# Macaron stack on one core: norms by log and exp inside the tick, rows turned one tick later, and a distance setup that overlaps its stacking

## The reference, cut to what matters

```python
Q = (x @ W_k.T).reshape(B, S, H, dk).transpose(0, 2, 1, 3)
squared_dist = sq_norm - 2.0 * dot + sq_norm.transpose(0, 1, 3, 2)
attn = softmax(-squared_dist * inv_sqrt_dk)
...
# one local layer, 8 heads of 64, windows of 64 that look one window back
q, k, v = split(shift_token(x) @ wqkv)
q = l2norm(q) * qs                  # l2norm: t / max(|t|, 1e-12)
k = l2norm(k) * ksc
q, k = rotary_xpos(q, k)            # rotation by position, with a growth
x = x + local_attention(q, k, v) @ wo
h = layernorm(shift_token(x)) * lg + lb
a, g = split(h @ w1 + b1)
x = x + (a * gelu(g)) @ w2 + b2
```

## Time and profile before

| | us |
|---|---|
| median of 3 runs | 3577.19 (3571.36 to 3577.69) |
| the profiled execution: its time | 3580.72 |
| its span in the trace | 3578.6 |
| TensorE, matmuls, busy | 3183.2 (89%) |
| VectorE, busy | 1976.4 (55%) |
| ScalarE, busy | 2167.5 (61%) |
| GpSimd, busy | 1737.4 (49%) |
| mean granted TensorE clock | 0.959 of full |

### The profile page before, as it was taken

How to read it: one execution, slowest core, us unless ns; L and a number is a source line. 1 busy time by engine, 2 the same in 40 slices (tenths; PEclk the granted TensorE clock), 3 DMA queues, 4 the chain that set the end, 5 groups by cost and what they waited for, 6 DMA issues and landing times. The chain is left out here.

```text
span 3578.6 us, 73165 instructions
## 1 busy us (share of the span) xinstructions
PE 3183.2 (89%) x26564; PEld 1951.8 (55%) x26564; DVE 1976.4 (55%) x4014; ACT 2167.5 (61%) x3580; POOL 1737.4 (49%) x1412
## 2 busy tenths in 40 slices
PE   6499999868999999749999999999998599999995
PEld 5222222435666666526666666666665366666663
DVE  4200000337777777545556555656565577777773
ACT  2399999526666666535555555555554366666663
POOL 1100000039889988523333333333332698998882
PEclk9699999979999999979999999999999799999998
DMA  1122222021111111100000000000000211111111
GB/s 33 20 36 39 36 38 38 7 74 34 35 36 38 37 36 34 25 10 9 7 6 9 6 9 6 9 6 9 6 6 4 86 37 35 37 37 37 35 33 36
DMA packets 124405, 95.70 MB, mean 27 GB/s; under 512 B 80448, under 2 KB 100544, under 8 KB 123968
## 3 DMA queue, kind: packets, MB, share of 16 engines
q1 hardware_dynamic: 122784, 89.41, 11.4%
q10 hardware_dynamic: 1440, 3.80, 0.3%
HBM read 22.90 MB, written 2.10 MB: 7 GB/s over the span
## 5 line engine op out<-in xcount | busy, mean ns | idle before, releaser
L1761 POOL TENSOR_SCALAR e<-e,inv 128x768 f32<-128x768 f32 (+7 forms) x512 | 375.3, 746 | 761.8 <-DVE inv L1653 761.8
L1724 ACT ACTIVATE e<-e,nmax 128x768 f32<-128x768 f32 (+7 forms) x512 | 395.4, 772 | 429.5 <-DVE e L1648 426.2
L1648 DVE TENSOR_SCALAR_CACHE_REDUCE e<-slot 128x768 f32<-128x768 f32 (+7 forms) x512 | 376.2, 754 | 243.8 <-PE slot L1537 243.8
L530 ACT ACTIVATE e<-slot 128x1024 f32<-128x1024 f32 x512 | 472.9, 1091 | 43.8 <-PE slot L466 43.8
L896 POOL TENSOR_TENSOR inv_norm<-floored,minus_half 128x16 f32<-128x16 f32 x128 | 374.1, 2922 | 10.7
L1641 DVE COPY eT<-slot 128x512 f32<-128x512 f32 (+3 forms) x384 | 238.7, 622 | 234.1 <-PE slot L1548 233.9
L1548 PE MATMUL slot<-ident,e 128*128 128x128 f32 x2304 | 332.7, 280 | 8.7 <-POOL e L1761 3.7
L1531 PE MATMUL slot<-key,q 64*128 64x512 f32 (+3 forms) x1536 | 318.1, 518 | 19.0 <-ACT v L1711 12.7
L889 POOL TENSOR_TENSOR rot<-cosine,sine 128x1024 f32<-128x1024 f32 x128 | 302.1, 2360 | 44.3 <-DVE sine L1228 44.3
L857 POOL TENSOR_TENSOR prob<-prob,inv_total 128x1024 f32<-128x1024 f32 x128 | 242.6, 1895 | 129.2 <-DVE inv_total L1246 129.2
L1548 PEld LDWEIGHTS slot<-ident,e 128*128 128x128 f32 x2304 | 252.5, 141 | 92.0 <-issue 68.9
(11 more groups left out here) (161 smaller groups left out, 6420.8 us busy)
## 6 DMA issues: line engine op xcount, KB each, us to landing
v_mix<-v SPq DMA_DIRECT2D x256, 128.0 KB, 2.3
w_qkv<-in_causal_w_dram SPq DMA_DIRECT2D x32, 192.0 KB
query<-q_hi SPq DMA_DIRECT2D x128, 32.0 KB
keys<-q_hi SPq DMA_DIRECT2D x128, 32.0 KB
query<-q_lo SPq DMA_DIRECT2D x128, 32.0 KB
keys<-q_lo SPq DMA_DIRECT2D x128, 32.0 KB
hs<-H SPq DMA_DIRECT2D x32, 128.0 KB
h1s<-H SPq DMA_DIRECT2D x32, 128.0 KB
```

What stands on the lines that cost most here:

```text
L530: act.activation(e[n % E_RING][:], c.slots[n % RING][:].rearrange(flat), ACT.Exp, scale=2 * SCALE).then_inc(e_ready, 1)
L1648: dve.tensor_scalar(e[n % RING][h][:, 0:cols], c.slots[h][:].rearrange(flat)[:, 0:cols], -1.0, None, ALU.mult, ALU.min, accum_out=nmax[:, ...
L1724: act.activation(part, part, ACT.Exp, bias=nmax[:, n, h:h + 1], scale=-1.0, accum_out=total[:, n, h:h + 1]).then_inc(e_ready, 1)
L1761: pool.tensor_scalar(part, part, inv[:, n, h:h + 1], 1.0, ALU.mult, ALU.mult).then_inc(scaled, 1)
```

## The change

In the local layers:

- The turn lags move: TQ from 2 to 1, PT from 3 to 2, OT from 4 to 3.
- The power on GpSimd goes. ScalarE takes Ln of the floored sums and then Exp of -1/2 times it, after its copy of v, and GpSimd corrects the result y0 with one Newton step: y0 * (1.5 - 0.5 * n * y0 * y0), four operations on 128x16.
- VectorE sums the squares ahead of the three table products, not after them.
- GpSimd multiplies by the inverse norms in the tile's own tick, right after the rotation sum.
- Of ScalarE's tables, the set with both Ln and Exp is loaded in place of Exp's.
- b2 is no longer added by GpSimd: it becomes a row of `w2`, with a hidden unit that is 0.0625 * gelu(16) = 1. The two loads of a broadcast b2 go.

In the distance setup:

- Normalisation, transposes and products of the 4 batches are in one block. The products for the columns (`q_hi`, `q_lo`) come ahead of those for the rows.
- SyncE issues the 40 stacking DMAs of batch 0, group 0 in that block: the 16 of `q_hi` when that is written, then 16 of `q_lo`, then 8 of the norms.

```diff
+            row_statistics(nc, c, moments=False)
             with nc.Block() as block:
+                @block.sync
+                def _(sp):
+                    heads = [stack_head(sp, stacked, 0, 0, j) for j in range(GROUP)]
+                    sp.wait_ge(cleared, 5)
+                    sp.wait_ge(hi_ready, 1)
+                    for high, _, _ in heads:
+                        high()
+                    sp.wait_ge(lo_ready, 1)
+                    for _, low, _ in heads:
+                        low()
+                    sp.wait_ge(norm_hi_ready, 1)
+                    sp.wait_ge(norm_lo_ready, 1)
+                    for _, _, norms in heads:
+                        norms()
...
+                    for b in range(B):
+                        columns(b)
+                        if b < B - 1:
+                            turn_rows(2 * b + 2)
+                            turn_rows(2 * b + 3)
+                        rows(b)
+                        norms(b)
...
-    TQ, PT, OT, FFN, DOWN = 2, 3, 4, 2, 3
+    TQ, PT, OT, FFN, DOWN = 1, 2, 3, 2, 3
...
+                def inverse_norms(a):
+
+                    first = first_inv[:, a.j % 2, :]
+                    pool.wait_ge(first_inv_ready, a.t + 1)
+                    if known(a.t, 1):
+                        pool.wait_ge(correction_ready, 2 * a.t)
+                    pool.tensor_tensor(inv_square[:], first, first, ALU.mult).then_inc(inv_square_ready, 1)
...
+                    pool.tensor_tensor(product[:], inv_square[:], floored[:, a.j % 2, :], ALU.mult).then_inc(correction_ready, 1)
...
+                    pool.tensor_scalar(correction[:], product[:], -0.5, 1.5, ALU.mult, ALU.add).then_inc(correction_ready, 1)
...
+                    pool.tensor_tensor(inv_norm[:, a.j % 2, :], correction[:], first, ALU.mult).then_inc(inv_norm_ready, 1)
...
-                def add_b2(a):
-                    pool.wait_ge(h1s_loaded, 80 * a.g + 80)
-                    rows = H[:, bass.ds(row(a.g), G), :]
-                    pool.tensor_tensor(rows, rows, b2[a.depth][:].unsqueeze(1).broadcast_to([P, G, P]), ALU.add)\
-                        .then_inc(b2_ready, 1)
...
-                    pool.tensor_tensor(inv_norm[:], floored[:], minus_half[:].broadcast_to([P, 2 * HEADS]), ALU.pow)\
-                        .then_inc(inv_norm_ready, 1)
...
                     for r in range(G):
                         if turned := tile(step, r, PT, depth):
                             scale(turned)
-                        if last := tile(step, r, 1, depth):
-                            unit_rows(last)
                         if r == 1 and (ffn := group(step, FFN, depth)):
                             deviations(ffn)
-                            add_b2(ffn)
                         if own := tile(step, r, 0, depth):
+                            floor_norms(own)
+                            inverse_norms(own)
                             rotated(own)
-                            inverse_norms(own)
+                            unit_rows(own)
...
+                def inverse_norms(a):
+                    act.wait_ge(floor_ready, 3 * a.t + 3)
+                    act.activation(log_norm2[:], floored[:, a.j % 2, :], ACT.Ln).then_inc(log_norm2_ready, 1)
+                    act.wait_ge(log_norm2_ready, a.t + 1)
+                    if known(a.t, 2):
+                        act.wait_ge(inv_norm_ready, a.t - 1)
+                    act.activation(first_inv[:, a.j % 2, :], log_norm2[:], ACT.Exp, scale=-0.5).then_inc(first_inv_ready, 1)
...
-                            act.preload_act_table(ACT.Exp)
+                            act.preload_act_table_set("natural_log_exp_and_others")
                         if own:
                             values(own)
+                            inverse_norms(own)
...
+    bias[:, 0, hid], bias[:, 1, hid] = 0.0625, 16.0
     down = np.zeros((n, chunks * P, P), w2.dtype)
-    down[:, :hid] = w2
+    down[:, :hid], down[:, hid] = w2, b2
```

More of the change, by code:

```diff
@@ L316, in _, with turn_rows, columns @@
                 def _(pe):
[L317 to L326, removed]
-                            m = pe.matmul(c.slots[2][0:HEADS, half, :], sel[:], sq[b % 2][:, half * 512:half * 512 + 512],
-                                          start=True, stop=True)
-                        m.then_inc(norm_ready, 1)
[L331 to L337, removed]
+                    def turn_rows(i):
+                        pe.wait_ge(xn_ready, G * (i + 1))
+                        if i >= 2:
+                            pe.wait_ge(columns_ready, i - 1)
+                        for j in range(G):
+                            m = pe.transpose(c.slots[3][:, i % 2, j * P:(j + 1) * P], xn[:, i % 2, j, :], c.ident[:])
+                        m.then_inc(turned, 1)
+                    def columns(b):
+                        pe.wait_ge(columns_ready, 2 * b + 2)
                         if b:
@@ L344, in _, with rows @@
                         m.then_inc(qT_ready, 1)
-                        if b == 0:
-                            pe.wait_ge(merged_ready, 1)
[L347 to L350, removed]
+                    def rows(b):
+                        if b:
+                            pe.wait_ge(q_out, b)
+                        for t in range(TPB):
+                            m = pe.matmul(c.slots[0][:, t // 4, (t % 4) * P:(t % 4 + 1) * P],
+                                          xT[:, (b * TPB + t) * P:(b * TPB + t + 1) * P], wk[:], start=True, stop=True)
+                        m.then_inc(q_ready, 1)
@@ new lines, in norms @@
+                    def norms(b):
+                        pe.wait_ge(sq_ready, b + 1)
+                        if b:
+                            pe.wait_ge(norm_hi_ready, b)
+                            pe.wait_ge(norm_lo_ready, b)
+                        else:
+                            pe.wait_ge(merged_ready, 1)
+                            pe.wait_ge(eff_out, 1)
+                        for half in range(2):
+                            m = pe.matmul(c.slots[2][0:HEADS, half, :], sel[:], sq[b % 2][:, half * 512:half * 512 + 512],
+                                          start=True, stop=True)
+                        m.then_inc(norm_ready, 1)
@@ L359, in _ @@
+                    columns(0)
+                    columns(1)
                     for b in range(B):
[L360 to L362 removed]
                         act.wait_ge(qT_ready, b + 1)
@@ L670, in local_layers @@
         small = [sb(f"small{l}", [P, 8]) for l in range(DEPTH)]
-        b2 = [sb(f"b2{l}", [P, P]) for l in range(DEPTH)]
         scales = [sb(f"scales{l}", [P, 2, 2, D]) for l in range(DEPTH)]
```

153 lines of the change are left out of this document (102 added, 51 removed).

## The result

| | before | after |
|---|---|---|
| median of 4 runs, us | 3576.22 (3571.36 to 3577.69) | 3646.91 (3645.54 to 3653.68) |
| span of the profiled execution, us | 3578.6 | 3645.8 |
| GpSimd busy, us | 1737.4 | 1440.1 |

The changed kernel takes 1.0204 times as long (95% interval 1.0186 to 1.0222): 71 us more. GpSimd does 297 us less, and the kernel is slower. The forecast of 3564 us, and its whole range of 3510 to 3610, were too low: the forecast by 83 us.

What follows compares the result with a forecast made beforehand. The prediction took GpSimd and TensorE as close, neither alone the limit, waiting for each other through VectorE and ScalarE, and the setup as serial. 3580.7 - 35.3 + 31 - 9 = 3567, the median 3.5 lower: 3564 us; range 3510 to 3610.

Steps and rivals of the forecast that it cites:

- fill and drain: Local streams' first eight ticks and end: -1.5 and -3 us a stream, together -9 us.
- Distance setup, -35.3: Setup of the distance attention: DMAs issued earlier, first score product at 132.0 and not 167.26, so -35.3 us.
- Rival (a): Local streams: GpSimd was the limit, so the step falls to TensorE's 42 us; 3460 us in all; chance 12%.
- r=0, 10.7: Local step's tick r=0, turn to turn: TensorE is the limit with the down products, 10.7 us as before.
- r=3, 11.3: Local step's tick r=3: v starts late behind ScalarE's gate 2 and table load, 11.3 us and not 10.25.
- r=1, 10.8: Local step's tick r=1: the turn now waits for GpSimd's queue and the norms, 10.8 us and not 8.07.
- The ring: Local tick's chain from unit rows through turn, copies, Ln, Exp, small operations and rotation sum to unit rows: 8.7 us unhindered.
- r=2, 13.2: Local step's tick r=2: z and its transposes come sooner, 13.2 us and not 15.06.
- rival (c): Local streams: TensorE's clock falls while waiting for the r=1 turn, 1.9 us a step, +49, 3613 us; chance 15%.
- Sum 46.0 against 44.8 on average: +1.2 a step: Local step: the four ticks add up to 46.0 us against 44.8, over 26 steps in both streams, +31 us.
- What the change puts in its place: Local streams: turning rows one tick later, not two, closes a ring within one tick; costed tick by tick, +31 us.
- rival (d): Local streams: the small operations are dearer, 0.8 us more at both r=1 and r=3, +42, 3606 us; chance 10%.

Runs made afterwards that it cites:

- e1: The changed kernel's new distance setup with the local layers of the kernel before: 3548.40 us, ratio 0.9921 to before.
- e7: e1 with b2 folded into w2 as a row, nothing else of the local change: 3500.90 us, ratio 0.9793 to before.
- e8: The changed kernel with the power back on GpSimd in place of Ln, Exp and the four operations: 3668.49 us, ratio 1.0259 to before.
- e2: The changed kernel with old lags 2, 3, 4, unit rows in the next tick, small operations behind the rotation sum: 3631.97 us, ratio 1.0160 to before.
- e10: e2 with Ln and Exp in ScalarE's idle times, GpSimd's floor ahead of unit rows, small operations heading the next tick: 3489.70 us, ratio 0.9761 to before.
- e9: e7 with VectorE's normalised rows of the batch after the next placed between q_lo and n_lo in the setup: 3498.18 us, ratio 0.9781 to before.
- e11: e10 with e9's early VectorE rows in the setup: 3486.79 us, ratio 0.9756 to before.
- e4: The changed kernel with the layer norm's five GpSimd operations moved behind the unit rows of r=1: 3600.78 us, ratio 1.0073 to before.
- e12: e4 with VectorE's moments moved from the end of r=0 to behind the rotation of r=1: 3572.63 us, ratio 0.9991 to before.
- e3: The changed kernel with 20 unread TensorE transposes ahead of its wait for unit rows in r=2: 3608.45 us, ratio 1.0097 to before.

## Why the prediction was wrong, by its own steps

**The result as a sum.** From e1: b2 folded -47.5 (e7), lags +167.6 (e8), norms by Ln, Exp and Newton -21.6 (after), and -27 for the setup: 71 more than before. The prediction had -35, +31 and -9. How the loss of the streams divides holds for this order of steps only: the new norms give 22 us with the short lags; with the old ones they cost 131 over e7 as e2 places them, and give 11 as e10 does. Of the 83 us that the forecast was off, some 8 are the setup, some 57 the 26 steps and some 19 the fill and drain.

**Distance setup, -35.3: right in kind, 8 us off.** The DMAs were in time, as said. "They fit, by 3 us only" failed: 6.6 us a batch was TensorE's own time, while a batch went through norms, `n_lo` and rows on VectorE. In e9, where the rows no longer stand behind `n_lo`, a batch takes 6.4 and the first score starts within 0.8 us of the forecast 132.0. Of the 35.3 us the stage's last score keeps 30.0 (e1), and the time 27.

**"GpSimd and TensorE ... neither is alone the limit": right.** Rival (a) had 3460 with GpSimd as the limit. Even e11, with GpSimd at 30 us a step, does not reach that. But (a) was nearer than its time says: with the old lags kept, less work on GpSimd brings the step to 42.44 us in e10, where (a) said 42.

**r=0, 10.7, and r=3, 11.3: right** (10.75 and 11.45). GpSimd's idle time ahead of `inv_square` in r=3 is 2.81 us, where some 4 was drawn.

**r=1, 10.8: 0.4 short** (11.16). The floor ends 15.7 us after the r=0 turn and not 15.5, and the unit rows start 2.50 us after the rotation sum and not 2.33. The ring was drawn in the right order: e4 and e12 each remove a thing that it named ahead of the unit rows, and TensorE's idle time falls from 3.03 to 1.13 and then to 0.64.

**r=2, 13.2: right without the clock.** e3, whose clock stays up, has z's transposes 4.74 us after the turn, gate 0 at 9.56 and 12.97 for the tick (forecast 4.9, 9.8 and 13.2). After has 5.91, 10.93 and 14.34. So the step that failed is the choice between the forecast and rival (c). It is the largest of those that failed, but not the only one: rival (c) with its own price still gave 3613. The mean step and the fill and drain, below, make most of the rest. The idle time before the turn was drawn as 2.8 us. The prediction gave the clock's fall 15%, for the reason that TensorE was 92% busy around it. Its own showed the fall after 2.87 us. The price of (c), 1.9 us, was too high (1.3 to 1.5); its place was right.

The loop itself had rows that bear on this more closely. Between the marks of groups 0 and 13 in the first stream of before the clock falls three times, once in this r=2 tick:

```profile
877.12 1.12 PE L1026 MATMUL slot<-ident,z 128*128 128x128 f32 x4 [2.81 <-DVE H L1251]
878.48 1.97 PE L989 MATMUL slot<-ident,prob 128*128 128x128 f32 x8 [0.24 <-POOL prob L857]
```

The four products take 1.12 us where 0.65 to 0.66 is usual, the eight 1.97 and not 1.09, and in the 44 us before them TensorE was busy 85%. In the third, at 1416, it had been busy 94% (41.14 of 44 us), and the idle times just before were 1.52 and 0.50 us. So a busy loop was no safety, and this could be read before the forecast. The Trainium skill, "TensorE: Matmul & The Clock Gate", section "HAM oscillation — how this bites in real kernels", warns of idle gaps inside a loop; its rule there speaks of longer ones than the 3.03 and 3.00 us before most falls here. The traces decide.

**"Sum 46.0 against 44.8 on average: +1.2 a step": an error of working.** 46.0 was drawn on the step of the earlier trace rows, which takes 44.12; 44.8 is a mean that holds longer steps too, and these stay longer after. Like with like it was +1.9, 49 us. The forecast would have been 3582, which is not faster than before. Measured is +3.58 in the middle step (47.70 against 44.12) and +88 us in 26 steps: 1.9 was drawn, 1.3 is the clock, and r=1 has most of the rest. So of the 57 us missed in the 26 steps 18 are this error and some 33 the clock.

**Fill and drain, -9: wrong.** From the last of the 13 steps to the last mark it is 4.3 us more than in e1 in the first stream and 5.6 in the second, not 3 less. A step in which no tile enters any more still has the ring: from mark 13 to 14 it is 48.47 us, and 41.29 in e1.

**"What the change puts in its place" was costed as one sum.** The gain of r=2 (-1.9) comes from b2 and the relief of GpSimd, the loss of r=1 from the lags, and that of r=3 from the lags and Ln behind v together (r=3 takes 10.24 us in e2, 10.45 in e8 and 11.45 in after). e7 shows that the first can be had without the second. The small operations cost what was said: Ln and Exp 0.22 us each, the four on GpSimd 0.20 to 0.22, so rival (d) falls.

## What to carry to other kernels

When a stage is shortened, draw what must now fit between two ends of one engine's wait, and price the idle time twice: once as a wait, and once for the lower clock behind it if that engine is TensorE. A short operation that waits for another engine costs all that is queued behind it: the norms cost 142 us more or less by their place in the lists of ScalarE and GpSimd alone (e2, e10). Before a forecast leans on a condition ("not in so busy a loop"), look for it in the whole stream, and not in one step. Take a change apart before you keep or drop it: this one is slower by 2.0%, and two of its parts alone, the setup and b2, are faster by 2.1%.

## What the hardware showed that I had not expected

TensorE's clock fell inside a loop in which it was busy nine tenths of the time, after one idle stretch of 3.03 us (after), 3.00 (e2) or 4.24 (e8). The length of the idle time alone does not tell when: in e4 it fell behind 1.85 us (the eight transposes at 1258.59 then take 1.84 us and not 1.09) and stayed at 1.00 behind 1.91 (at 1172.16), and in after it stayed there behind 3.03 (at 1229.09). In the middle steps it stayed at 1.00 after 1.13 (e4) and 0.64 us (e12). In the setup, VectorE's normalisation of eight 128x128 tiles took 4.16 us (0.52 a tile) while GpSimd cleared the stacked tiles beside it, and 2.14 (0.27 a tile) after that; GpSimd's 1024-column clears took 1.09 us then and 0.94 or 0.95 at other times. That one slows the other is only argued from this; no run took the clears away. The Trainium skill, "SBUF — State Buffer", section "Terms", says that the two engines share a pair of ports to the memory, which would fit.
